# Expert layers with full float32 up products: weights fetched slot by slot, middle rows produced turned

## The reference

```python
# layer 1 (twice): 8 experts, top 2, gated
probs = softmax(x @ gate_w.T);  w, idx = top_k(probs, 2);  w = w / sum(w)
g, u = split(x @ gate_up_proj[e].T, 2)            # 128 -> 2 x 512
out += w_e * ((silu(g) * u) @ down_proj[e].T)     # 512 -> 128
# layer 2 (twice): 8 experts, top 2, and one shared expert that every token takes
shared = silu(x @ shared_w1.T) @ shared_w2.T
out = shared + sum_e gate_e * (silu(x @ experts_w1[e].T) @ experts_w2[e].T)
```

## Time and profile before

| what | us |
|---|---|
| median of three runs | 3575.4 |
| the runs | 3574.93, 3575.40, 3579.01 |
| the profiled execution | 3567.43 |
| its span, first to last instruction | 3565.3 |
| PE busy | 3055.0 (86% of the span) |
| DVE busy | 2421.9 (68%) |
| ACT busy | 2133.5 (60%) |
| POOL busy | 1222.4 (34%) |
| bytes moved by DMA | 187.15 MB, mean 52 GB/s |

### The profile page before, as it was taken

The page is one execution under the profiler, slowest core; times in us unless marked ns, Lnnn a source line. Parts: engine busy times, 40 slices in busy tenths (PEclk is TensorE's granted clock), DMA queues, the critical chain, the costliest instruction groups (busy, mean ns, idle before and its releaser), DMA issues. The chain is left out here.

```text
span 3565.3 us, 61688 instructions
## 1 busy us (share of the span) xinstructions
PE 3055.0 (86%) x20359; PEld 1919.6 (54%) x20359; DVE 2421.9 (68%) x6667; ACT 2133.5 (60%) x3201; POOL 1222.4 (34%) x1338
## 2 busy tenths in 40 slices
PE   4669999786658967999999779689778987998999
PEld 3533333344447852222222368668756875886787
DVE  7778988576964458999999454454586455656565
ACT  4448989664534545999999735433434344653564
POOL 4454551121546642010010276466536660001000
PEclk9879999998878988999999979899999998999999
DMA  1053440000021122010000321221202122000100
GB/s 58 1 165 112 126 130 18 1 1 24 0 118 40 48 86 89 21 30 21 21 30 2 132 72 48 79 106 46 82 7 93 46 75 80 1 1 10 59 10 12
DMA packets 87166, 187.15 MB, mean 52 GB/s; under 512 B 23169, under 2 KB 41409, under 8 KB 83793
## 3 DMA queue, kind: packets, MB, share of 16 engines
q1 hardware_dynamic: 60048, 117.66, 9.8%
q0 software_dynamic: 26816, 65.58, 5.9%
HBM read 121.23 MB, written 61.34 MB: 51 GB/s over the span
## 5 line engine op out<-in xcount | busy, mean ns | idle before, releaser
L2598 ACT ACTIVATE core_pr<-core_two 128x1024 f32<-128x1024 f32 (+3 forms) x896 | 787.5, 934 | 49.5 <-PE core_two L2565 45.8
L2634 DVE TENSOR_REDUCE core_mx<-core_one 128x1 f32<-128x512 f32 x778 | 491.4, 683 | 20.9 <-PE core_one L2517 13.7
L2577 PE MATMUL core_ps_o<-core_pr,core_vals 128*32 128x512 f32 (+3 forms) x3584 | 434.1, 559 | 1.7 <-ACT core_oT L2609 1.5
L2517 PE MATMUL core_one<-arena,queries 64*128 64x512 bf16 (+3 forms) x1472 | 375.3, 363 | 29.2 <-PEq L62 19.0
L2565 PE MATMUL core_two<-queries,arena 64*128 64x512 bf16 (+3 forms) x1792 | 341.4, 360 | 9.5 <-ACT core_pr L2598 6.8
L2517 PEld LDWEIGHTS core_one<-arena,queries 64*128 64x128 bf16 x1472 | 113.2, 94 | 297.0 <-DVE core_mx L2634 132.2
L2451 POOL COPY core_vals<-arena 128x288 f32<-128x288 f32 x32 | 14.7, 459 | 690.4 <-PE core_ps_o L2577 690.4
L2628 DVE CUSTOM_DVE_ANT_0 core_junk<-core_one,core_over 128x512 bf16<-128x512 f32 (+4 forms) x334 | 201.7, 644 | 26.3 <-PE core_one L2517 21.9
L2565 PEld LDWEIGHTS core_two<-queries,arena 64*128 64x128 bf16 x1792 | 94.3, 94 | 201.7 <-ACT core_pr L2598 145.4
L2604 ACT ACTIVATE core_over<-core_two 128x1024 f32<-128x1024 f32 (+4 forms) x167 | 159.9, 958 | 58.3 <-PE core_two L2540 45.6
L110 DVE CAST moe_second_x_hi<-moe_second_bank 128x128 fp32r<-128x128 f32 x142 | 41.4, 292 | 217.6 <-PE moe_second_bank L573 217.6
(11 more groups left out here) (656 smaller groups left out, 8030.2 us busy)
## 6 DMA issues: line engine op xcount, KB each, us to landing
arena<-expert_out SPq DMA_DIRECT2D x64, 256.0 KB, 3.6
expert_rows<-arena SPq DMA_DIRECT2D x13, 512.0 KB, 8.1
core_w_raw<-in_m_up POOLq DMA_DIRECT2D x25, 256.0 KB, 3.3
m_hi<-core_w_hi POOLq DMA_DIRECT2D x25, 256.0 KB, 2.4
m_lo<-core_w_lo POOLq DMA_DIRECT2D x25, 256.0 KB, 3.0
q_parts<-qkv_parts SPq DMA_DIRECT2D x16, 384.0 KB, 2.6
k_parts<-qkv_parts SPq DMA_DIRECT2D x16, 384.0 KB, 3.4
queries<-q_parts SPq DMA_DIRECT2D x64, 96.0 KB
```

The source lines that it names most:

```text
L2517: pe.matmul(one[bank[e]][:, 0:width], q_sb[rows, hq, pair, qt * P:(qt + 1) * P], k_sb[rows, hq, pair, kc * CW:kc * CW + width], start=True ...
L2577: mm = pe.matmul(ps_o[h * 32:(h + 1) * 32, off:CW], vals[:, hq % 2, j, h, :], pr[:, (n * N2 + k) % KEPT, h // 2, h % 2, off:CW], start=(j ...
L2598: a.activation(pr[:, step % KEPT, i, :, off:CW], two[spot[e] % 2][:, :, off:CW], ACT.Exp, scale=HD ** -0.5).then_inc(s_wide, 1)
L2634: v.tensor_reduce(at, scores, AX.X, ALU.max).then_inc(s_read, 1)
```

## The change

The four expert stages no longer hold the up weights on chip. SP reads a slot's expert offset from `woff` with a register load and fetches the raw float32 weights of that expert from the input in DRAM, into a ring of six (`chosen`), a slot at a time. PE uses those weights as the stationary operand, in 128 x 128 blocks, and the turned x as the moving operand with 128 columns, as plain float32. The output is hidden x rows, which `down` can use directly, so that `turn_h`, its copies, and the halving of x go; DVE makes one copy of the turned x. `psY` becomes a pair of banks, `hT` a ring of four. In shared stages the units of the shared expert are placed otherwise (14 before the slots, then one in every third slot), the normalising, turning and copying of x moves into the gaps of the table's rounds, and gathers are issued eight slots ahead, one for each scatter. POOL no longer cuts the 25 pieces of up weights in the first attention core.

```diff
@@ gathers_behind: one rule for both kinds of stage
-    early = 19
-    if s < early:
-        return min(12 + 2 * (s + 1), s + 24)
-    return min(SLOTS, early + 23 + (s - early + 1) * 2 // 3)
+    return min(SLOTS, 8 + s + 1)
...
+    HT, WB = 4, 6
+    xrT = st.sb("xrT", [P, 2, P])
+    chosen = st.sb("chosen_w", [P, WB, halves, HID])
...
-    A, B, psH = (bank[0:2], (bank[2], bank[7]), bank[4:6]) if gated else (bank[4:6], None, bank[6:8])
-    psX, psY = bank[3], bank[6] if gated else bank[2]
+    A, B, psY = (bank[0:2], (bank[2], bank[7]), bank[4:6]) if gated else (bank[4:6], None, bank[6:8])
+    psX = bank[3]
...
-    CHOOSING, PLACING, ASIDE, BEHIND = (1, 3, 1, 2) if shared else (0, 0, 0, 0)
+    CHOOSING, PLACING, ASIDE, BEHIND = (2, 3, 1, 2) if shared else (0, 0, 0, 0)
+    AT, EVERY = 4, 3
+    TURNED_AT = (1, 2, 5, 6)
+    ADDED = {7: 3, 19: 4, 31: 5, 43: 6, 52: 7}
@@ SP
-            for part, t in zip(parts, (up_hi, up_lo)):
-                for f in range(halves):
-                    cols = slice(f * W, (f + 1) * W)
-                    sp.dma_start(t[:, cols], part[:, cols]).then_inc(s_wl, 16)
...
             if prefetch:
                 prefetch(sp)
+            by_half = up_all[:, 0:halves * W].rearrange("p (f n) -> p f n", f=halves)
+            sp.wait_ge(s_chain, WOFF)
+            for s in range(SLOTS):
+                e = sp.value_load(woff[0:1, s:s + 1], min_val=0, max_val=7 * HID)
+                if s >= WB:
+                    sp.wait_ge(s_up, s - WB + 1)
+                sp.dma_start(chosen[:, s % WB], by_half[:, :, bass.ds(e, HID)]).then_inc(s_wc[s % WB], 16)
@@ PE, before the slots
             always(CHOOSING)
-            for c in range(2, 4):
-                turn_xn(c)
             pe.wait_ge(s_chain, TOTAL)
...
             always(PLACING)
-            for c in range(4, CHUNKS):
+            for c in range(2, 4):
                 turn_xn(c)
...
                 mm.then_inc(s_table, 1)
+                if n in TURNED_AT:
+                    turn_xn(4 + TURNED_AT.index(n))
@@ PE, the slots
             def up(s):
-                pe.wait_ge(s_xlo, s + 1)
+                pe.wait_ge(s_xc, s + 1)
+                pe.wait_ge(s_wc[s % WB], 16 * (s // WB + 1))
...
-                    mm = product(pe, out[s % 2][:], (x_hi[:, s % 2, :], x_lo[:, s % 2, :]),
-                                 [t[:, half * W:(half + 1) * W][:, bass.ds(at[s], HID)] for t in (up_hi, up_lo)])
+                    for j in range(4):
+                        mm = pe.matmul(out[s % 2][:, j * P:(j + 1) * P], chosen[:, s % WB, half, j * P:(j + 1) * P],
+                                       xrT[:, s % 2, :], start=True, stop=True)
...
-                if 1 <= s <= SLOTS:
-                    turn_h(s - 1)
-                always(1)
+                if s % EVERY == 0:
+                    always(1)
                 if s >= 2:
                     down(s - 2)
@@ ACT, before the slots
-            for i in range(2, GROUPS_T):
-                normalise(i)
             always(CHOOSING)
+            normalise(2)
+            if not shared:
+                normalise(3)
+            always(PLACING)
             for c in range(2, 4):
                 copy_xn(c)
-            always(PLACING)
-            for c in range(4, CHUNKS):
-                copy_xn(c)
-            always(BEFORE - CHOOSING - PLACING)
+            if shared:
+                for n in range(GROUPS_T * TOPK):
+                    if n in TURNED_AT:
+                        copy_xn(4 + TURNED_AT.index(n))
+                    if n + 1 < GROUPS_T * TOPK:
+                        always(ASIDE)
+                    if n < GT // 2:
+                        normalise(3, range(2 * n, 2 * n + 2))
+            always(BEHIND)
@@ DVE, the slots
-                upper(v, x_hi[:, s % 2, :], psX[:, 0:P]).then_inc(s_xhi, 1)
-                v.wait_ge(s_xhi, s + 1)
-                lower(v, x_lo[:, s % 2, :], psX[:, 0:P], x_hi[:, s % 2, :]).then_inc(s_xlo, 1)
+                v.tensor_copy(xrT[:, s % 2, :], psX[:, 0:P]).then_inc(s_xc, 1)
...
-            def copy_h(s):
-                v.wait_ge(s_ht, s + 1)
...
-                v.tensor_copy(hT[:, s % 2, :], psH[s % 2][:]).then_inc(s_hc, 1)
@@ build: only the last layers' weights are cut in the first attention core
-        m1_parts, m2_parts, f3_parts = parts("m1", d["m1_up"].shape[1]), parts("m2", d["m2_up"].shape[1]), parts("f3", F3)
+        f3_parts = parts("f3", F3)
```

115 lines of the change are left out of this document (45 added, 70 removed).

## The result

| | before | after |
|---|---|---|
| median, us | 3575.16 (3572.54 to 3579.01, 4 runs) | 3530.82 (3526.65 to 3537.15, 4 runs) |
| ratio of the times, 95% interval | | 0.9877 (0.9858 to 0.9895) |
| the profiled execution, us | 3567.43 | 3532.92 |
| its span, us | 3565.3 | 3531.1 |
| bytes moved by DMA | 187.15 MB | 254.13 MB |

The medians are 44.3 us apart, against 45.0 predicted. The two profiled executions are only 34.5 apart, and that needs a word first, since all else is read from them.

The account below looks back on a forecast made before the run. PE was taken to bound the slots before, POOL the shared slots after. Gated stages -7.6, shared stages -36.2 and first attention core -1.2 sum to -45.0 us, giving 3530.4 us; the forecast's own range is 3520 to 3541, the wider one 3516 to 3560.

Parts of the forecast that it names:

- The likeliest case: Whole kernel: 45.0 us gained, to a median of 3530.4 us; chance 0.52, own range 3520 to 3541.
- Gated slot: PE in gated slots: 25 instructions at 0.111 us, 2.78 instead of 2.85 us, 5.1 us less over 71 slots.
- Start of the gated stages: First fetch of weights in gated stages: first up 4.8 us after WOFF, 2.4 us later than before.
- POOL as the bound of the shared slots: Shared slots: POOL needs 2.57 us per pair, 183.1 us to the last scatter; gains 13.6 and 15.1 us.
- Before the shared slots: PLACED to first gather in shared stages: 25.3 us with the new order, 3.0 and 4.5 us less.
- gated pace: Bound for the time before the shared slots, at a gated stage's pace: 4.2 and 5.7 us less.
- First attention core: POOL no longer cuts up weights beside the head groups: 1.2 us less, at most 1.4.
- The fetch in the loop: Weight fetches in the slots, priced at nothing: DMA busy 2.03 of 2.78 us gated, 1.23 of 2.57 shared.
- POOL isn't the bound: Rival for the shared stages: a pair takes less than 2.47 us, 10 us less in each, 3510 us; chance 0.05.
- its instructions slow down beside the fetches: Rival: POOL's indirect DMAs slow beside weight fetches, 26 us for each 0.1 us, 3557 us; chance 0.12.
- the DMA engines bound the gated slots: Rival: at 180 GB/s a gated slot takes 3.34 us, 80 us more, 3611 us; chance 0.08.
- PE falls to 1.2 GHz in the last shared slots: Rival: slots of 3.8 us for about 11 slots, at most 27 us, up to 3557 us; chance 0.04.

Follow-up runs that it names:

- the second pair of traces: The kernels before and after, both unchanged, run again on one chip: 3570.03 and 3527.40 us, ratio 0.9887.
- experiment 1: Kernel after, but only the first six weight fetches of each stage are made: 3527.5 us; gated stages 210.3 and 211.3, shared 183.9 and 184.2.
- experiments 4 to 6: Kernel after with the old order before the shared slots (whole, or ACT's half), two slots of weights instead of six, or cutting put back: 3691.4 to 3716.9 us.
- the two old orders: Kernel after with PE's and ACT's old order before the shared slots, and with ACT's early normalising alone: 3701.8 and 3705.5 us.

## Why the prediction was right, point by point

The likeliest case came: 44.3 us gained against 45.0, and each of its terms with the right sign. The closeness of the totals is partly luck: terms missed by 1.1 to 1.3 us in both directions, the rows of the kernel before came from an execution in which PE's clock made the two second stages 2.2 and 1.2 us longer than in the other trace, and the same terms taken from the second pair of traces sum to -38.8 us, 6 short of the prediction.

*Gated slot.* 2.78 predicted, 2.79 measured. Before, it was 2.85 in the first gated stage, from which I took it, and 2.83 in the second, whose slots therefore had 0.9 us less to gain. That a full product costs what the same form costs at `down` held, weights just landed or resident.

*Start of the gated stages.* The mis-sized term. First up 4.8 us after WOFF predicted, 5.66 and 5.22 measured: SP took 1.04 us to issue where I had 0.7, and from there to the first up it took 4.6 and 4.2 us where I had 4.1. From the first up to the last scatter it is 208.9 us before and 203.1 after, 5.8 less, where my terms give 6.2. So the gated stages gained 2.5 and 2.7 us, not 3.8. The estimate by the Trainium skill, DMA: Bandwidth & Descriptors, section Anatomy of one DMA, was 3.2 us for 512 KB and 2.6 for 256 KB. The page gives its fit for DMAs that GpSimd issues; the fetches here are SyncE's. The trace has 4.1 in the loop, 4.5 and 4.1 for the first 512 KB of the two gated stages, and 2.9 for 256 KB: near the estimate for the small one, 1.3 to 1.4 times it for the large one.

*POOL as the bound of the shared slots.* Right in its mechanism and in nearly every number: 183.1 predicted, 183.5 and 183.6 measured. The 0.4 us are scatter 1. Shown by three runs that move it both ways: a quarter less of POOL's instructions gives 174, PE's bound; the same PE work denser gives 192; two gathers moved into POOL's own wait, together with expert offsets that are ready 0.8 us sooner, leave POOL no wait at all and give 180.7.

*Before the shared slots.* 25.3 us predicted, 24.2 measured (24.7 and 24.6 run again), the bound that I had named "gated pace". I kept 1.1 us for DVE's two additions in the rounds, and they turned out to be hidden. The old order, put back, takes 28.1 and 28.4 us, where the kernel before has 28.3 and 29.8, and 28.2 and 28.6 run again.

*First attention core.* 1.2 predicted, 0.9 in the traces, 1.0 by the run that puts the pieces back.

*What was priced at nothing.* The fetch in the loop (experiment 1: nothing). `all_down(13)`: PE waits 1.66 us for DVE's addition in front of it, and the weights of slot 0 land 0.6 us after that work is done, so it is hidden, narrowly. PE's clock stays at 1.00 in the late shared slots of this trace, where PE is busy 35.1 of 40 us.

*The rivals.* That POOL isn't the bound, that its instructions slow down beside the fetches and that the DMA engines bound the gated slots are refuted, the last with room to spare: 383 GB/s can be had where 227 are drawn. But the way in which I added up DMA time was wrong, by 0.5 us in a doubled slot; it did no harm only because the real limit was farther off. That PE falls to 1.2 GHz in the last shared slots did happen once, in the first shared stage of the kernel after run again: about 2528 us its runs of eight instructions take 1.73 and 1.92 us instead of 1.06. It cost nothing, for the stage has 183.5 us as before.

## What to carry to other kernels

When a change makes one engine's part shorter, list the next engine's instructions in the stretch and count them at their start-to-start distance, issue included: 62 pairs and 7 single scatters of POOL gave the time from scatter 1 to the last to 0.1 us. Price a fetch in two places, its rate in the loop and its first landing: here the rate cost nothing and the landing ate 3.3 of 5.8 us in the first gated stage, part of which comes back when the first fetch is issued earlier and in two halves. Compare single executions stretch by stretch, since the clock after PE's pauses moved one of them by 6.6 us outside the change; and where a stretch starts behind such a pause, read its clock first, since it moved stages by up to 2.2 us. The engine that is busy throughout needn't be the bound: PE was busy throughout in most of the shared slots, and POOL, which waited for nothing, set the end.

## What was not expected of the hardware

**Pauses on some chips.** The runs of experiments 4 to 6 shared one chip, and the second one with a ring of two ran on another; there every kernel took longer: in the traces, which are of the kernel after and its variants, all of it lies in the slots. On the first the kernel before took 3675.1 us, 100 more than elsewhere (3685.8 on the second), the two old orders 3701.8 and 3705.5, the ring of two 3697.1 (3716.9 on the second), and the kernel after with the cutting put back 3691.4, so that the gain of 44 us had become a loss of 16, of which the cutting explains 1. The window of its gated slots, and one pause in full:

```profile
1092.00:1285.00 193.00, 167.16 (x1400) 163.91 (x1401) 51.36 (x119) 47.57 (x110) 105.57 (x108) 0.96 0.64 196
```

```profile
1151.90 0.27 PE L573 MATMUL moe_first_bank<-ident,arena 128*128 128x128 f32 x1
1152.01 1.06 PE L596 MATMUL moe_first_bank<-arena 128*128 x8
1152.65 0.97 POOL L459 DMA_INDIRECT arena<-expert_rows,moe_first_row_index  x1 [0.30 <-issue]
1154.71 0.29 DVE L823 COPY moe_first_xrT<-moe_first_bank 128x128 f32<-128x128 f32 x1 [4.41 <-remote]
1154.80 0.28 ACT L694 ACTIVATE arena<-moe_first_bank 128x128 f32<-128x128 f32 x1 [2.40 <-remote]
1155.06 2.05 PE L587 MATMUL moe_first_bank<-moe_first_xrT,moe_first_chosen_w 128*128 128x128 f32 x16 [1.99 <-DVE moe_first_xrT L823]
```

DVE copies the turned x 0.3 us after PE starts to turn it in every other slot; here it takes 2.8 us, and ACT, which waits for another product of PE, comes 0.1 us later. In 19 of the 71 slots of that stage the copy comes so late, by 0.6 to 2.5 us, ten times 13.4 us after the late copy before it, which is four slots; together that is 39 us. In the shared stages late copies come in a pattern that repeats mostly every 9.2 to 9.3 us, which is three slots. They come only in the slots of the expert stages, and the same kernel, traced twice elsewhere, has none. What holds PE's signals back isn't shown by any row. I had supposed PE's instruction loads: elsewhere, from 1092 to 1285 us, the kernel before loads 14 pieces and the kernel after 16, but the pieces don't fall at a fixed distance from the pauses, and 14 to 16 doesn't give 25 to 41 us a stage, a quarter of the 100 and of the 163 us by which the two kernels are longer there. No trace of the kernel before was taken on such a chip, so whether it pauses at the same places is open. What can be said is that the ratio of 0.988 was measured twice without pauses, and that with them the one comparison there is, of one execution each, gives 1.004, for the kernel after with the cutting put back.

**DMA.** Busy shares of the DMA engines aren't additive: 0.73 at 227 GB/s, 1.05 at 383. And a gather's landing grows from 2.5 to 4.3 us beside fetches of 512 KB per slot, while the time that POOL spends on it stays at 0.97. Why the share grows more slowly than the rate isn't shown by any run.
